# Moving the build of the one-hot behind the first subtraction, and the scaling of the gathered rows right behind the exponents

## The reference

```python
h_trans = features @ Watt_w.T + Watt_b
e_raw = jnp.sum(h_trans[dst] * jnp.tanh(h_trans[src] + e_r), axis=-1, keepdims=True)
e_ij = leaky_relu(e_raw / 8)
exp_e = jnp.exp(e_ij - segment_max(e_ij, dst)[dst])
alpha = exp_e / (segment_sum(exp_e, dst)[dst] + 1e-09)
h_neigh = segment_sum(features[src] * alpha, dst)
h_out = leaky_relu((features + h_neigh) @ W1_w.T + W1_b + (features * h_neigh) @ W2_w.T + W2_b)
out = layernorm(features + h_out)
```

## Time and profile before

| | |
|---|---|
| time of three runs | 2823.59, 2827.87, 2828.71 us, median 2827.87 |
| profiled execution, time | 2813.21 us |
| profiled execution, span | 2811.4 us |
| granted clock of TensorE | 0.508 of full speed |
| busy: PE, DVE, ACT, POOL | 1365.9 (49%), 1652.8 (59%), 1602.6 (57%), 1655.3 us (59%) |
| DMA | 296.07 MB, mean 105 GB/s |

### The profile page before, as it was taken

One profiled execution on the slowest core, in us unless ns is written; L12 is line 12 of the kernel. 1 busy time (PEld: TensorE's weight loads), 2 busy tenths in 40 slices (PEclk: granted clock), 3 DMA queues, 4 the chain that ended last, 5 costly groups with the idle time before them and its releaser, 6 DMA issues. The chain is left out here.

```text
span 2811.4 us, 32328 instructions
## 1 busy us (share of the span) xinstructions
PE 1365.9 (49%) x6440; PEld 1096.9 (39%) x6440; DVE 1652.8 (59%) x7936; ACT 1602.6 (57%) x2794; POOL 1655.3 (59%) x1670
## 2 busy tenths in 40 slices
PE   4344444455444444554445444554544555444455
PEld 4333343344333433443334334443433444333344
DVE  2256666655665656565666555655666556566567
ACT  2345555565555555565655556655555565656565
POOL 4466666666665666566666656666566666666660
PEclk7555555555555555555555555555555555555555
DMA  4333333333333333333333333333333333333331
GB/s 162 113 94 101 108 109 108 108 107 97 109 101 107 108 108 108 108 95 105 105 108 109 108 108 100 116 100 100 104 108 109 108 102 102 110 100 108 108 111 31
DMA packets 169270, 296.07 MB, mean 105 GB/s; under 512 B 111730, under 2 KB 111942, under 8 KB 169107
## 3 DMA queue, kind: packets, MB, share of 16 engines
q1 hardware_dynamic: 114689, 185.75, 19.9%
q0 software_dynamic: 53152, 107.98, 15.5%
q10 hardware_dynamic: 1266, 0.93, 0.1%
HBM read 284.43 MB, written 10.07 MB: 105 GB/s over the span
## 5 line engine op out<-in xcount | busy, mean ns | idle before, releaser
L628 POOL DMA_INDIRECT got<-table,src_i x1631 | 1625.7, 997 | 1074.5 <-DVE spare L1290 515.4
L949 PE MATMUL ps_hd<-hw,hotT 128*128 128x64 f32 x3322 | 731.9, 421 | 7.3 <-ACT hotT L735 7.3
L949 PEld LDWEIGHTS ps_hd<-hw,hotT 128*128 128x128 f32 x3322 | 721.9, 333 | 7.5 <-ACT hotT L735 7.5
L994 PE MATMUL ps_acc<-parts,hot 128*128 128x195 bf16 x1661 | 328.3, 364 | 637.9 <-DVE parts L1303 567.2
L750 ACT ACTIVATE edge<-edge 128x256 f32<-128x256 f32 (+1 forms) x444 | 176.6, 398 | 613.8 <-issue 499.8
L994 PEld LDWEIGHTS ps_acc<-parts,hot 128*128 128x128 bf16 x1661 | 208.8, 136 | 744.9 <-issue 619.8
L724 ACT ACTIVATE off<-dst_all,node 128x1024 bf16<-128x1024 int32 x222 | 424.7, 1913 | 121.3 <-remote 73.6
L1303 DVE TENSOR_TENSOR parts<-spare,parts 128x520 bf16<-128x520 f32 x222 | 147.1, 663 | 235.1 <-ACT parts L790 211.8
L1232 DVE CUSTOM_DVE_ANT_0 edge<-edge,ps_hd 128x64 f32<-128x64 f32 x1661 | 265.8, 217 | 18.8 <-remote 7.1
L1005 PE MATMUL ps_misc<-ident,sum_prod 128*128 128x128 f32 x111 | 52.4, 472 | 431.7 <-DVE sum_prod L1319 431.7
L735 ACT ACTIVATE hotT<-off,ones 128x1024 f32<-128x1024 bf16 x222 | 242.6, 1093 | 7.2
(11 more groups left out here) (137 smaller groups left out, 1974.1 us busy)
## 6 DMA issues: line engine op xcount, KB each, us to landing
dst_all<-in_dst SPq DMA_DIRECT2D x109, 960.5 KB
edge<-in_edge_attr SPq DMA_DIRECT2D x110, 480.0 KB
got<-table,src_i POOLq DMA_INDIRECT x1631
table<-hx SPq DMA_DIRECT2D x12, 512.0 KB
hw<-table SPq DMA_DIRECT2D x111, 32.0 KB
xw<-in_x SPq DMA_DIRECT2D x111, 32.0 KB
out<-y_out SPq DMA_DIRECT2D x111, 32.0 KB
x_piece<-in_x SPq DMA_DIRECT2D x3, 768.0 KB, 4.4
```

The costliest lines, as they stand in the source:

```text
L628: pool.indirect_dma_start(got[b.four][:, g, 0:2 * D], None, table, bass.IndirectOffsetOnAxis(ap=src_i[b.four][:, g:g + 1], axis=0))\
L949: last = pe.matmul(expanded(g, c), hotT[b.two][:, g, :], hw[b.two][:, :], start=True, stop=True)
L994: last = pe.matmul(a_parts, hot[b.four][:, g, :], parts[:, g, :, :].rearrange("p a d -> p (a d)"), start=(g == 0), stop=(g == tiles(b) - 1))
```

## The change

On DVE, `place` is cut in two. The copy of the node's number (`set_node`, for `nxt`, on which ACT's L724 waits) now stands ahead of the exponents. The rest of `place` and the four instructions of `build_hot` no longer run for `nxt` but for the step's own block `b`, and they stand behind `left_part` and ahead of `dot` 1. `scale_rows` so follows directly on the exponents. PE gets a wait in `sum_edges`: it now asks that `hot` of its block is built. The lists of ACT, POOL and SP are unchanged.

```diff
@@ PE, sum_edges @@
                 pe.wait_ge(rest_low[p], b.n + 1)
+                pe.wait_ge(hot_built[PIECE_CHUNKS[p][-1]], b.n + 1)
                 for g in range(*piece(b, p)):
@@ DVE @@
-            def place(b):
-
-                dve.wait_ge(dst_in[b.four], (b.fours + 1) * 16)
-                if follows(b, 1):
-
-                    dve.wait_ge(hot_built[NC - 1], b.n)
+            def set_node(b):
+
                 if follows(b, 2):
 
                     dve.wait_ge(consts, 5)
                     dve.wait_ge(off_set[NP - 1], b.n - 1)
                 column = node_all[:, b.n:b.n + 1] if b.known else node_all[:, bass.ds(b.n, 1)]
                 dve.tensor_copy(node[b.two][:, :], column).then_inc(node_set, 1)
+
+            def place(b):
+
+                dve.wait_ge(dst_in[b.four], (b.fours + 1) * 16)
+                if follows(b, 1):
+
+                    dve.wait_ge(hot_built[NC - 1], b.n)
                 column = base_all[:, b.n:b.n + 1] if b.known else base_all[:, bass.ds(b.n, 1)]
@@ DVE, step @@
                 if exists(b):
                     add(b, 0)
+                if exists(nxt):
+                    set_node(nxt)
                 if exists(prev):
                     exponents(prev)
-                if exists(nxt):
-                    place(nxt)
-                    for c in range(NC):
-                        build_hot(nxt, c)
-                if exists(prev):
                     scale_rows(prev, 0)
                     scale_rows(prev, 1)
...
                     left_part(prev, 0)
                     left_part(prev, 1)
                 if exists(b):
+                    place(b)
+                    for c in range(NC):
+                        build_hot(b, c)
                     dot(b, 1)
                     add(b, 2)
```

## The result

The changed kernel takes 3098.86 us (four runs, 3089.53 to 3108.36) against 2828.29 for the kernel before beside it: a ratio of 1.096, interval 1.0924 to 1.0996. The profiled execution has a span of 3087.8 us at a granted clock of 0.513. It is slower by 9.6% where a gain of 3% was forecast. On another chip the same pair gave 1.078 (1.0665 to 1.0888).

The account below looks back on a forecast made before the run. No engine is full; a loop of waits bounds it, POOL's batch plus pause. Pause 4.52 + batch 18.79 to 19.26 gives 23.54 us against 24.40, 89 us less over 104 steps: 2738 us, range 2600 to 2870.

Parts of the forecast that it names:

- The hold belongs to a time and not to L1199: DVE's 4.13 us idle before L1199 runs roughly from T0 to the last gathers' landing; whoever is next pays.
- Scaling 1.98 us earlier, and then `src_i` decides: DVE's scaling comes 1.98 us earlier, POOL then waits for its ids; some 0.4 to 0.75 us come through.
- pause 4.52 and batch 18.79 to 19.26: POOL's step: pause between batches plus gather batch, 23.31 to 23.78 us, middle 23.54, against 24.40.
- `hot` costs no gather, and its 1.9 us go into L1303's wait for ACT: Mid-step `hot` on DVE doesn't slow gathers; most of 1.9 us hides in L1303's 2.15 us wait, 0.3 left.
- It fits into 23.5 us if the hold ends 7.1 us after T0 ... that is where it settles: DVE's turn is hold + 1.7 + 14.7 us after T0; the hold takes up its slack and POOL's loop decides.
- the first sign of being wrong: The hold moves ahead of T0, seen as idle time <-remote before L1261, the old L1257.
- The early hold: Hold begins before DVE's scans are through; 27.26 us once in four steps gives 2835 us; chance 0.25, 0.17 slower.
- The port rival: DVE's L1199 can't start while gathers run and waits out each batch; some 12 us a step, 4080 us; chance 0.02.
- The copy of the node and PE's wait: DVE's 0.15 us copy ahead of the exponents and PE's added wait for `hot` were each to cost nothing.

Follow-up runs that it names:

- e8: Changed kernel with the scaling put back behind the bias and the sums of `before`, `hot` still built mid-step; 1.107 of the kernel before.
- e1: Changed kernel with `hot` built for `nxt` right behind the early scaling, ahead of the bias; 2899.0 us to 2771.72 for the kernel before.
- e3: Changed kernel building `hot` for only one tile of each chunk from the fifth block on, work left out; 1.074 of the kernel before.
- e12: Changed kernel loading 258 destination ids instead of 1921 in L500's broadcast from the fifth block on, work left out; 1.078 of the kernel before.
- e5: Changed kernel in which POOL also waits for DVE's row scan ahead of the ninth gather of a batch; 1.0035 of the kernel before.

## Why the prediction was wrong, point by point

*The hold belongs to a time and not to L1199*: right. L1294 ran without it, and the hold came to others. What the hold is was missing: late increments, and they hit whoever waits for one.

*Scaling 1.98 us earlier, and then `src_i` decides*: right as to the releaser (74 waits; L1294 released no batch of the steady part), wrong in the size. This is the term of the sum that was mis-sized: pause 4.52 and batch 18.79 to 19.26 were to make 23.54. In the step shown the batch takes 18.48 us, and the pause 10.21 (10.5 on the mean of 74). The pause of 4.52 us held for a batch that ended 4.5 us after T0. The long steps have T0 4.7 us behind the batch; there the ids are issued late and take 3.86 us from issue to start instead of 2.37, and the pause is 10.2.

*`hot` costs no gather, and its 1.9 us go into L1303's wait for ACT*: right, the wait is gone (204.4 to 12.2 us). But I took that wait for free room, and e8 against e1 shows that the order without it is the worse one (1.107 against 1.04 to 1.05).

*"It fits into 23.5 us if the hold ends 7.1 us after T0 ... that is where it settles"*: this is the step that failed. It took the hold as bound to T0 with a fixed length and DVE's list behind it as unhurt. The window closes by the row of gathers, about 2.5 us behind its end, and not by T0. It opened after 8.8 us instead of 14.9 (medians), lay over L960 to L1261, and DVE stood 469.8 us there and 235.8 before the dots. So T0 itself came late, and with it the ids and POOL's restart. That is the first sign of being wrong that the prediction named, idle time <-remote before L1261.

*The rivals.* The early hold was named with its place, the idle time before L1261 ahead of T0, and its price of 27.26 us for a step. The measured mean of 27.07 is near that by chance: the steps are spread from 17 to 41 us, and one of 82 is between 26.5 and 27.5. The rival was given 0.25, and I let it come once in four steps, for 2835 us, since 92 waits before L1199 stood against ten at the scan. That counted how often the old order had met it, and the new one moves just that. The port rival is out: L1203, the old L1199, waits 58.7 us in 11 cases and not 12 us a step. The copy of the node and PE's wait cost nothing that the trace shows.

*Open*: why at the same pace of 1.25 us the window opens after 14.9 us in one order and 8.8 in the other. In the kernel before it opens with T0 in most steps (0.2 to 1.3 us behind it in the middle half), in the changed one it doesn't (13 to 16.5 us behind the T0 before it in the middle half), so T0 is not what opens it. e3 and e12 speak against the length of `hot` and the large transfer; e1 and e8 point to the stretch in which DVE no longer waits for L790 and PE sums 14 tiles in one go instead of 8 and 6, but that was not varied by itself. Nor did a run show what it is that delays the increments, and why none of ACT's is late.

## What to carry to other kernels

An idle time "<-remote" whose producer has long ended can be a late increment. Compare the producer's end with the waiter's start before calling it a property of the waiting line, and look for what runs at that time on every engine. If such a window hangs on a stream of gathers, then a reordering moves the window over other waits as well, so the question is which chain of increments it will lie over. Here the chain from DVE to PE and back was the costly one: with the window moved off it e5 had no loss, though more increments were late. And a wait that an order leaves in the middle of a step is not free room to fill until a run has shown it.

## What the runs showed of the hardware

In rows of gathers of 128 rows each, 1.25 us from one to the next, semaphore increments of PE and DVE arrive late: up to 8.5 us in the kernel before, up to 29.5 us in the changed one (8.3 us in the row shown). No recorded increment of ACT was late. In such windows issues of SP and waits of POOL take 0.70 to 0.72 us and start 1.4 us and more apart. With waits between the gathers that made it 1.49 us from gather to gather some 20 of 4400 increments were late, at 1.60 none. Twelve waits that were already met, put behind each gather, made either order 5% faster than the kernel before.
